# Four-layer network on one core: who issues the first row of maxima, what the first loads of an attention wait for, and when the first tokens of the grouped block are loaded

## The chip, the cores and the metric

The kernel runs on one core of a Trainium2 chip. The metric is the device time of one execution in microseconds (us); lower is better. Times of the kernel before are the median of three runs. The profile is of one further execution, and its times count from the first instruction of the span.

## The reference, cut to what matters

Four layers work on x of 4096 tokens by 128 (16 batches of 256 tokens). Each layer adds the result of an attention-like block and of an expert block to x. The change touches the attentions of the second and third layer, called att1 and att2 in the kernel, and the expert block that is run inside att1.

```python
# both attentions: 16 heads of 8
scores = einsum('bhqd,bhkd->bhqk', q, k) * scale      # att1: causal, att2: not
p = softmax(scores)
out = (einsum('bhqk,bhkd->bhqd', p, v)) @ Wo + bo
# experts beside att1: top 2 of 9
scores = sigmoid(x_flat @ gate.T + bias); top_scores, selected = top_k(scores, 2)
out += cw[:, e] * ((silu(x @ ew1[e].T) * (x @ ew3[e].T)) @ ew2[e].T)
```

## The kernel before, in words

**Stages.** Both attentions are one function, `attention`. First `projections` makes q and k in 8 chunks of 512 tokens (chunk ch holds batches 2ch and 2ch+1): TensorE multiplies, VectorE and ScalarE (ACT) split each value into three bf16 parts in a ring of PB = 4 buffers, and the queue of SyncE (SP) stores the parts of each chunk to DRAM (`q_parts`, `k_parts`, L1834), two DMAs a chunk. Their landing is counted in `stored[ch % 4]`. Between these stores, from chunk 2 to chunk 5, SP issues `early_load`: the loads of batches 0 and 1.

**Loads.** `load(b)` brings the parts of batch b back, rows arranged for TensorE: 12 DMAs (L1983 and L1985, two halves of six), into one of BUFS = 4 buffers of `qs` and `ks`.

**Steps.** The main loop has a step for each pair of heads, 8 steps a batch (PAIRS = 8), from step -12 (LEAD = 12). TensorE's step i does `scores(i)` (L2156), `maximum(i + 12)` (L2131, L2138 with the causal mask) and the product with the values of an earlier step (L2180). VectorE reduces the scores of `maximum` to row maxima (L2313 causal, L2317 not). When the 8 steps of a batch are reduced, the maxima are split in two bf16 parts, turned by TensorE (L2214) and copied by ACT to `mt` (L2295, which counts `mt_ready`). Two DMAs, together called `top(b)`, then write them into two rows of `qs` on either half (L2074), and `scores(8b)` waits for both. ACT's exponent (L2272) follows each `scores`. So before step 0 TensorE needs `top(0)`; at step 4 it needs `load(2)`, at step 12 `load(3)`.

**SP's program in the main loop** is in order: the last stores, a wait for the landing of the stores of all chunks (L1841), `load(2)`, `top(0)`, then for each batch b `top(b + 1)`, for b = 0 `load(3)`, a wait until the scores of batch b are done, and `load(b + 4)`.

**The grouped block.** In att1 the tokens are scattered by expert to `disp` by GpSimd (POOL), 64 indirect DMAs (L913). When step 32 is reached (MID = 32), all engines turn to the 72 tiles of `grouped`: SP loads a tile of 128 tokens into one of two buffers `xin` (L1177), TensorE turns it (L1226 and L1228 for tiles 0 and 1, L1190 for the rest), multiplies it with the weights of its expert (L1197), turns the gated product (L1219) and multiplies again (L1206). TensorE's order is up(0), then for each tile j: up(j + 1), turn of tile j + 2, turn of h(j), down(j - 1). SP loads tile j + 2 when tile j is turned. In SP's program this stands in the round b = 3, behind `top(4)` and `load(7)`. In att2 a dense expert block stands at MID; its code is not touched.

**What shares memory.** The buffers of `projections` are given free before `pr`, `ot` and the like are laid out, so nobody may write those before the last stores have landed. Before, SP's wait at L1841 gives this, since nothing else of the main loop can pass `top(0)`.

Of the kernel before, what the change touches and what calls it, by code (L numbers as in the profile page):

```python
# [13 lines left out]
P = 128  # L14
# [3 lines left out]
NT = N // P  # L18
# [1131 lines left out]
def grouped(nc, g, s, sb, disp, ybuf, r, w13, w2):  # L1150


    NJ = TILES1
    xin = sb("xin", [P, 2, D])
# [7 lines left out]
    def each(eng, body):  # L1162
# [6 lines left out]
        body(NJ - 2, NJ // 2 - 1, 0, 2, 1)  # L1169
        body(NJ - 1, NJ // 2 - 1, 1, 2, 0)  # L1170

    def sync(sp):
        sp.wait_ge(r.scattered, 2 * NT * 16)

        def body(j, it, p, before, after):
            sp.wait_ge(s.turned, j + 1)
            sp.dma_start(xin[:, p, :], disp[bass.ds(j * P, P), :]).then_inc(x_in[p], 16)  # L1177
        each(sp, body)

    def tensor(pe):  # L1180
        pe.sem_inc(s.turned, 2)
# [115 lines left out]

    job = Names()
    job.sync, job.tensor, job.scalar, job.vector, job.gpsimd = sync, tensor, scalar, vector, gpsimd
    return job  # L1300


# [516 lines left out]
def projections(nc, g, s, sb, w, b, q_parts, k_parts, early_load):  # L1819
# [3 lines left out]
    NCH = N // CH  # L1823
    EARLY, PB = 2, 4
# [5 lines left out]
    def sync(sp):  # L1830
        for ch in range(NCH):
            sp.wait_ge(s.p_low, ch + 1)
            for m, out in ((0, q_parts), (1, k_parts)):
                sp.dma_start(out[:, :, ch * CH:(ch + 1) * CH].rearrange("a r t -> r a t"),  # L1834
                             parts[:, ch % PB, 3 * m:3 * m + 3]).then_inc(stored[ch % PB], 16)
            if ch == EARLY:
                sp.wait_ge(stored[0], 32)
            if EARLY <= ch < EARLY + 4:
                early_load(sp, (ch - EARLY) // 2, (ch - EARLY) % 2)
        for p in range(PB):  # L1840
            sp.wait_ge(stored[p], len(range(p, NCH, PB)) * 32)  # L1841

    def tensor(pe):
        pe.wait_ge(s.p_w_in, 64)
# [71 lines left out]

    job = Names()
    job.sync, job.tensor, job.vector, job.scalar = sync, tensor, vector, scalar
    return job


def attention(nc, g, title, prologue, project, wv, bv, wo, bo, q_parts, k_parts, causal, scale, moe=None, disp=None,
# [7 lines left out]
    BUFS = 4  # L1930
# [19 lines left out]
    with section(nc, title, *names, *PROJECT, "w_in", "filled", "ones_set", "consts", "biased", "qk_in0", "qk_in1", "qk_in2", "qk_in3",  # L1950
# [109 lines left out]

        steps = range(-LEAD, NP + PAIRS)

        with nc.Block() as block:

            @block.sync
            def _(sp):
                def load(b):
                    for half in range(2):
                        load_half(sp, b, half)

                def top(b):
                    sp.wait_ge(s.mt_ready, b + 1)
                    for half in range(2):
                        sp.dma_start(qs[half * HR + KR:half * HR + KM, b % BUFS],  # L2074
                                     mt[half * 2 * PAIRS:(half + 1) * 2 * PAIRS, b % 2, :]
                                     ).then_inc(mx_in[b % 2], 16)

                parts.sync(sp)
                load(2)
                top(0)  # L2080
                for b in range(BATCH - 1):
                    top(b + 1)
                    if b == 0:
                        load(3)
                    if b == 1 and dense:
                        job.weights(sp)
                    if b + BUFS < BATCH:
                        sp.wait_ge(s.s_ready, (b + 1) * PAIRS)
                        load(b + BUFS)
                    if (moe or dense) and (b + 1) * PAIRS == MID:  # L2090
                        job.sync(sp)

# [168 lines left out]
            def _(act):  # L2261
# [17 lines left out]
                for step in steps:  # L2279
# [11 lines left out]
                    if 0 <= b + 1 < BATCH and j == TURN:  # L2291
                        act.wait_ge(s.turned_nm, b + 2)
                        if b >= 1:
                            act.wait_ge(mx_in[(b + 1) % 2], (b - 1) // 2 * 32 + 32)
                        nc.scalar.copy(mt[:, (b + 1) % 2, :], g.ps[0:4 * PAIRS, MISC, 0:T]).then_inc(s.mt_ready, 1)  # L2295

            @block.vector
            def _(dve):
# [576 lines left out]
```

## Time and profile before

| | |
|---|---|
| median of three runs | 2017.84 us (2017.4 to 2018.54) |
| the profiled execution | 2014.04 us, its span 2012.1 us |
| TensorE | busy 1563.5 us, 78% of the span |
| VectorE, ACT, GpSimd | 67%, 52%, 40% of the span |
| att1, from its projections to its end, with the grouped block | about 857 to 1368 us |
| att2, the same, with the dense block | about 1386 to 1750 us |

A row of a timeline gives the start, how long the row lasts, engine, line, operation, output and inputs, and how many instructions are merged into it; in brackets stand the idle time ahead of it and what ended it. SPq is the queue of SyncE: the time of its row is that of issuing, not of moving the data. Tiles are named att_ in both layers.

### The profile page before, as it was taken

How to read it: one execution, taken by the hardware profiler on the slowest of the kernel's cores; microseconds unless marked ns; L12 is line 12 of the kernel's file. 1: busy time of each engine (PE TensorE's matmuls, PEld its weight loads, DVE VectorE, ACT ScalarE, POOL GpSimd, SP SyncE). 2: the span in 40 equal slices, each digit the busy share in tenths (PEclk: the TensorE clock that was granted, in tenths of full speed). 3: DMA queues.
4: the chain of work that ended last, by engine and by line, in shares of the span. 5: the costliest groups of instructions: out<-in, count | busy, mean ns of one | idle time of the engine just before them, and what ended most of it. 6: DMA issues, size and time to landing. Idle time of an engine off the chain costs nothing. (4 is left out here: it accounts for less than half of the span.)

```text
span 2012.1 us, 35698 instructions
## 1 busy us (share of the span) xinstructions
PE 1563.5 (78%) x12141; PEld 1070.2 (53%) x12143; DVE 1340.9 (67%) x2371; ACT 1045.9 (52%) x1858; POOL 799.5 (40%) x803
## 2 busy tenths in 40 slices
PE   5986887887866567457788889994589999649994
PEld 5753665665644444425566666662245444437883
DVE  7537777787899998685433348868762699436334
ACT  1468778787754454144333336664354577434440
POOL 1575556555688885276011124331500000024005
PEclk9997999999987888578899999997689999769997
DMA  5211111110010010565311115522651242111322
GB/s 149 93 62 51 55 45 34 50 50 29 19 31 25 24 24 9 214 201 106 55 43 44 43 39 91 87 40 70 131 86 55 38 66 37 54 51 40 100 69 78
DMA packets 153319, 130.35 MB, mean 65 GB/s; under 512 B 18929, under 2 KB 137864, under 8 KB 152914
## 3 DMA queue, kind: packets, MB, share of 16 engines
q1 hardware_dynamic: 140626, 104.57, 21.1%
q0 software_dynamic: 12544, 23.82, 4.5%
q8 instruction: 90, 1.47, 0.3%
q14 instruction: 59, 0.48, 0.1%
HBM read 77.08 MB, written 52.43 MB: 64 GB/s over the span
## 5 line engine op out<-in xcount | busy, mean ns | idle before, releaser
L662 POOL TENSOR_TENSOR xn_t<-xn_t,scan_du 128x512 f32<-128x512 f32 x256 | 321.5, 1270 | 179.0 <-ACT xn_t L804 101.3
L707 PE MATMUL banks<-scan_hc,ident 128*128 128x256 f32 x1024 | 297.4, 417 | 73.7 <-DVE scan_hc L859 73.5
L853 DVE TENSOR_TENSOR_SCAN xn_t<-banks,xn_t 128x512 f32<-128x512 f32 x256 | 311.5, 1217 | 41.3 <-ACT banks L794 35.0
L2272 ACT ACTIVATE att_pr<-banks 128x768 f32<-128x768 f32 (+1 forms) x256 | 234.3, 916 | 139.2 <-PE banks L2164 80.3
L794 ACT ACTIVATE banks<-delta,scan_exp_centre,a_neg 128x255 f32<-128x255 f32 x512 | 265.2, 559 | 47.3 <-DVE xn_t L853 47.0
L707 PEld LDWEIGHTS banks<-scan_hc,ident 128*128 128x128 f32 x1024 | 194.1, 208 | 136.2 <-DVE scan_hc L859 101.7
L859 DVE TENSOR_TENSOR scan_hc<-xn_t,banks 128x512 f32<-128x512 f32 x256 | 175.8, 687 | 28.1 <-PE banks L692 16.1
L2317 DVE TENSOR_REDUCE att_mb<-banks 128x4 f32<-128x1024 f32 x128 | 154.0, 1222 | 25.0 <-PE banks L2131 20.2
L913 POOL DMA_INDIRECT disp<-xn_tok,places x128 | 135.3, 1057 | 86.0 <-issue 61.2
L2180 PE MATMUL banks<-att_pr,att_vx 128*32 128x256 f32 (+1 forms) x2048 | 155.0, 376 | 4.9 <-ACT att_ot L2277 3.5
L2313 DVE TENSOR_REDUCE att_mb<-banks 128x6 f32<-128x768 f32 x128 | 121.6, 956 | 40.1 <-PE banks L2138 38.2
L2131 PE MATMUL banks<-att_ks,att_qs 48*128 48x256 bf16 (+1 forms) x1024 | 112.9, 278 | 38.4 <-DMA att_ks<-k_parts 33.9
L804 ACT COPY xn_t<-banks 128x512 f32<-128x512 f32 x128 | 74.6, 583 | 129.8 <-PE banks L683 125.0
L1103 POOL IOTA route_rev<- 128x16 f32 (+2 forms) x3 | 0.4, 143 | 342.0 <-SPq L1119 316.6
L1197 PE MATMUL banks<-grouped_w,att_xt 128*128 x288 | 106.3, 493 | 32.6 <-DVE att_h L1267 31.9
L2156 PE MATMUL banks<-att_qs,att_ks 50*128 50x256 bf16 (+1 forms) x1024 | 109.3, 270 | 25.2 <-DMA att_qs<-att_mt 23.0
L1293 POOL DMA_DIRECT2D ybuf<-att_yo x72 | 38.8, 539 | 214.0 <-DVE att_yo L1274 209.9
L1241 ACT ACTIVATE att_a<-banks 128x352 f32<-128x352 f32 x72 | 33.4, 463 | 153.6 <-PE banks L1197 153.6
L1261 DVE COPY att_xt<-banks 128x128 f32<-128x128 f32 x72 | 20.9, 292 | 126.1 <-PE banks L1190 117.0
L1482 POOL DMA_INDIRECT gau_gb<-ybuf,rows x32 | 33.3, 1040 | 125.7 <-PEq L1623 119.0
L1197 PEld LDWEIGHTS banks<-grouped_w,att_xt 128*128 128x128 f32 x288 | 50.0, 193 | 62.3 <-issue 47.5
L2156 PEld LDWEIGHTS banks<-att_qs,att_ks 50*128 50x128 bf16 x1024 | 40.0, 95 | 80.7 <-issue 40.5
(342 smaller groups left out, 3348.1 us busy)
## 6 DMA issues: line engine op xcount, KB each, us to landing
scan_ew<-f_packed SPq DMA_DIRECT2D x12, 578.0 KB, 4.2
q_parts<-att_p_parts SPq DMA_DIRECT2D x16, 384.0 KB, 4.1
k_parts<-att_p_parts SPq DMA_DIRECT2D x16, 384.0 KB, 6.0
att_qs<-q_parts SPq DMA_DIRECT2D x64, 96.0 KB
att_ks<-k_parts SPq DMA_DIRECT2D x64, 96.0 KB
gau_ew<-f_packed SPq DMA_DIRECT2D x8, 578.0 KB, 4.1
disp<-zeros SPq DMA_DIRECT2D x1, 4608.0 KB, 15.9
att_xin<-disp SPq DMA_DIRECT2D x72, 64.0 KB, 1.8
```

What stands on the lines that cost most here:

```text
L662: nc.gpsimd.tensor_tensor(bu[:, i % RING], b_sb[:, q % 2], du[:, b % 2, c:c + 1, :].to_broadcast([P, 2, T]), ALU.mult).then_inc(s.bu_made, 1)
L707: ins = nc.tensor.matmul(bank(Y_BANK)[:, c, :], g.ident[:], hc[:, i % RING, n, :], start=False, stop=(i % (PAIRS * DC) == PAIRS * DC - 1 a ...
L794: ins = nc.scalar.activation(bank(DA + i % RING)[:, n, 1:T], delta[:, c, b * T + 1:(b + 1) * T], ACT.Exp, scale=a_neg[:, c, state:state + ...
L853: v.tensor_tensor_scan(rows(h[:, i % 2]), g.ps[:, DA + i % RING, :], rows(bu[:, i % RING]), 0.0, ALU.mult, ALU.add).then_inc(s.scan_done, 1)
L859: v.tensor_tensor(hc[:, i % RING], h[:, i % 2], bank(C_BANK), ALU.mult).then_inc(s.hc_ready, 1)
L913: pool.indirect_dma_start(disp, bass.IndirectOffsetOnAxis(ap=r.scat_i[:, k, i:i + 1], axis=0), src[:, i, :], None, bounds_check=disp.shape ...
L1197: ins = nc.tensor.matmul(g.ps[:, 4 * p + 1 + m, 0:H1], xt[:, p, :], rows(w13[:, bass.ds(e, 1), m * H1:(m + 1) * H1]), start=True, stop=True)
L2156: ins = nc.tensor.matmul(g.ps[:, 2 * s_slot(i) + half, k * T:k * T + T - q0], ks[rows_of, p, j, k * P:(k + 1) * P], qs[rows_of, p, j, q0:T ...
L2180: ins = nc.tensor.matmul(g.ps[r * 32:(r + 1) * 32, O_BANK, q0:T], vx[:, b % 2, k, 4 * jg + r, :], pr[:, i % RING, half, k * T:k * T + T - q0],
L2272: nc.scalar.activation(pr[:, i % RING], g.ps[:, at:at + 2, 0:W], ACT.Exp, scale=scale).then_inc(s.p_ready, 1)
L2313: v.tensor_reduce(mb[:, b % 2, j, :].rearrange("p (g n) -> p g n", g=2), g.ps[:, at:at + 2, 0:W].rearrange("p g (n k) -> p g n k", k=P), A ...
L2317: v.tensor_reduce(mb[:, b % 2, j, :], g.ps[:, at:at + 2, :].rearrange("p g (n k) -> p (g n) k", k=T), AX_X, ALU.max).then_inc(s.m_taken, 1)
```

## The change

In both attentions ACT issues `top(0)` itself, behind its copy that makes `mt` of batch 0, and then waits until the stores of all chunks have landed. SP no longer waits for all stores: ahead of each `load(b)` with even b it waits for the stores of chunk b / 2 alone. In att1 SP loads tiles 0 and 1 of the grouped block in the round b = 2 (behind `load(6)`, once all scattered rows have landed), and in the round b = 3 only the loop for tiles 2 to 71 is left.

```diff
+    def first_tokens(sp):
+        sp.wait_ge(r.scattered, 2 * NT * 16)
+        for j in range(2):
+            sp.dma_start(xin[:, j, :], disp[j * P:(j + 1) * P, :]).then_inc(x_in[j], 16)
+
     def sync(sp):
-        sp.wait_ge(r.scattered, 2 * NT * 16)
-
-        def body(j, it, p, before, after):
+        def body(j, p):
             sp.wait_ge(s.turned, j + 1)
             sp.dma_start(xin[:, p, :], disp[bass.ds(j * P, P), :]).then_inc(x_in[p], 16)
-        each(sp, body)
+
+        with sp.Fori(1, NJ // 2) as it:
+            for p in range(2):
+                body(it * 2 + p, p)
...
-        for p in range(PB):
-            sp.wait_ge(stored[p], len(range(p, NCH, PB)) * 32)
+
+    def chunk_stored(eng, ch):
+        eng.wait_ge(stored[ch % PB], (ch // PB + 1) * 32)
+
+    def all_stored(eng):
+        for ch in range(NCH - PB, NCH):
+            chunk_stored(eng, ch)
...
+        def top(eng, b):
+            eng.wait_ge(s.mt_ready, b + 1)
+            for half in range(2):
+                eng.dma_start(qs[half * HR + KR:half * HR + KM, b % BUFS],
+                              mt[half * 2 * PAIRS:(half + 1) * 2 * PAIRS, b % 2, :]).then_inc(mx_in[b % 2], 16)
...
                 def load(b):
+                    if b % 2 == 0:
+                        parts.chunk_stored(sp, b // 2)
                     for half in range(2):
                         load_half(sp, b, half)
...
                 parts.sync(sp)
                 load(2)
-                top(0)
                 for b in range(BATCH - 1):
-                    top(b + 1)
+                    top(sp, b + 1)
                     if b == 0:
                         load(3)
...
                         load(b + BUFS)
+                    if moe and (b + 2) * PAIRS == MID:
+                        job.first_tokens(sp)
                     if (moe or dense) and (b + 1) * PAIRS == MID:
                         job.sync(sp)
...
                         nc.scalar.copy(mt[:, (b + 1) % 2, :], g.ps[0:4 * PAIRS, MISC, 0:T]).then_inc(s.mt_ready, 1)
+                        if b == -1:
+                            top(act, 0)
+                            parts.all_stored(act)
```

## Rows read from the trace of the kernel before

**Rows 1.** The page, its head.

```profile
span 2012.1 us, 35698 instructions
```

**Rows 2.** The waits of TensorE in att1 (857 to 1368): total, times, longest.

```profile
PE banks L2131 <- DMA att_ks<-k_parts: 17.4, 3, 11.9
...
PE banks L2156 <- DMA att_qs<-att_mt: 10.7, 1, 10.7
PE banks L1226 <- DMA att_xin<-disp: 9.1, 1, 9.1
```

**Rows 3.** The same view of att2 (1386 to 1750).

```profile
PE banks L2156 <- DMA att_qs<-att_mt: 12.3, 2, 9.2
```

**Rows 4.** Timeline of SP's queue at the start of att1.

```profile
896.08 1.24 SPq L1834 DMA_DIRECT2D k_parts<-att_p_parts  x1
903.11 0.32 SPq L1983 DMA_DIRECT2D att_qs<-q_parts  x1
...
908.62 16.16 SPq L2074 DMA_DIRECT2D att_qs<-att_mt  x4
```

**Rows 5.** Timelines of ACT and of TensorE there: end of step -1, step 0, step 4.

```profile
900.48 0.36 ACT L2295 CAST att_mt<-banks 32x256 bf16<-32x256 f32 x1 [10.40 <-PE banks L2214]
...
902.73 0.37 PE L2138 MATMUL banks<-att_ahead_k,att_half_eye 64*128 64x128 bf16 x4
913.81 0.39 PE L2156 MATMUL banks<-att_qs,att_ks 50*128 50x256 bf16 x2 [10.70 <-DMA att_qs<-att_mt]
...
920.77 0.22 PE L2131 MATMUL banks<-att_ks,att_qs 48*128 48x128 bf16 x2
```

**Rows 6.** Timelines of SP's queue, ACT and TensorE at the start of att2.

```profile
1428.50 0.31 SPq L1983 DMA_DIRECT2D att_qs<-q_parts  x1
...
1434.62 14.76 SPq L2074 DMA_DIRECT2D att_qs<-att_mt  x4
...
1427.11 0.36 ACT L2295 CAST att_mt<-banks 32x256 bf16<-32x256 f32 x1 [10.83 <-PE banks L2214]
...
1428.70 0.61 PE L2131 MATMUL banks<-att_ks,att_qs 48*128 48x256 bf16 x4
1438.53 0.61 PE L2156 MATMUL banks<-att_qs,att_ks 50*128 50x256 bf16 x4 [9.22 <-DMA att_qs<-att_mt]
```

**Rows 7.** Timelines of SP's queue and of TensorE's weight loads: `top(1)` of att1.

```profile
923.51 1.26 SPq L2074 DMA_DIRECT2D att_qs<-att_mt  x2
...
926.17 0.10 PEld L2156 LDWEIGHTS banks<-att_qs,att_ks 50*128 50x128 bf16 x2 [0.20 <-DMA att_qs<-att_mt]
```

**Rows 8.** Timeline of all engines where the grouped block starts.

```profile
968.14 0.30 SPq L1983 DMA_DIRECT2D att_qs<-q_parts  x1
...
969.49 0.42 DVE L2382 TENSOR_TENSOR x_tok<-x_tok,banks 128x256 f32<-128x256 f32 x1
...
972.99 20.27 SPq L1177 DMA_DIRECT2D att_xin<-disp  x8
...
978.53 0.45 PE L1226 MATMUL banks<-ident,att_xin 128*128 128x128 f32 x1 [9.08 <-DMA att_xin<-disp]
...
979.71 5.06 PE L1197 MATMUL banks<-grouped_w,att_xt 128*128 x8 [0.52 <-DVE att_xt L1261]
...
984.56 0.37 PE L1190 MATMUL banks<-ident,att_xin 128*128 128x128 f32 x1
...
988.22 1.45 PE L1197 MATMUL banks<-grouped_w,att_xt 128*128 x4 [0.26 <-DVE att_h L1267]
```

**Rows 9.** Windows of 1 us: busy time by engine, then PEclk, DMA share, GB/s.

```profile
901.00:902.00 1.00, 1.00 (x10) 0.87 (x4) 1.00 (x2) 0.00 (x0) 0.70 (x2) 0.50 0.61 218
...
971.00:972.00 1.00, 0.00 (x0) 0.00 (x0) 0.00 (x0) 0.00 (x0) 0.00 (x0) 0.55 0.77 81
```

**Rows 10.** Timelines of GpSimd and SP's queue: the last scatter, the end of `load(6)`.

```profile
946.30 0.97 POOL L913 DMA_INDIRECT disp<-xn_tok,places  x1 [0.30 <-issue]
...
960.28 0.31 SPq L1985 DMA_DIRECT2D att_ks<-k_parts  x1
```

More of the change, by code:

```diff
@@ L1299, in grouped @@
     job.sync, job.tensor, job.scalar, job.vector, job.gpsimd = sync, tensor, scalar, vector, gpsimd
+    job.first_tokens = first_tokens
     return job
@@ L1918, in projections @@
     job.sync, job.tensor, job.vector, job.scalar = sync, tensor, vector, scalar
+    job.chunk_stored, job.all_stored = chunk_stored, all_stored
     return job
@@ L2067, in load @@
                 def load(b):
+                    if b % 2 == 0:
+                        parts.chunk_stored(sp, b // 2)
                     for half in range(2):
                         load_half(sp, b, half)
[L2071 to L2076, printed above, removed]
                 parts.sync(sp)
                 load(2)
-                top(0)
                 for b in range(BATCH - 1):
-                    top(b + 1)
+                    top(sp, b + 1)
                     if b == 0:
```

## The prediction, as it was written before the result was known

> **What bounds the kernel now.** I read the page first: TensorE is the busiest engine, at 78% (the table above), so time is gained only where it stands idle in the stages that the change touches, and then only as much as nothing later takes back. [rows 1] gives the span against which the sum is made. Then the waits of TensorE by stage. In att1 three waits for a transfer stand out: 17.4 us for the loads of keys (11.9 of it ahead of the first maxima), 10.7 us in one piece for the row of maxima `top(0)`, and 9.1 us in one piece for the first tokens of the grouped block [rows 2]. In att2 the wait for `top(0)` is 9.2 us [rows 3]. The change aims at the 10.7, the 9.1 and the 9.2: 29.0 us at most, 1.4% of the span. The reader is to see that each is a single hole on the engine that sets the pace, so a us taken out of it is a us of the end, until the next wait is met.
>
> Then the timelines around each hole, to see what the transfer itself was late for. In att1 ACT has `mt` ready at 900.48 + 0.36 = 900.84, and TensorE is through with step -1 at 903.1 [rows 5]. SP issues the last store until 897.32, waits for its landing, issues `load(2)` from 903.11, and only behind its 12 DMAs `top(0)` at 908.62; the row merges it with `top(1)` [rows 4]. TensorE goes on at 913.81. So of the hole, 7.8 us are SP being late to issue (908.62 - 900.84), and 5.2 us are issue and landing. In att2 the same: ready at 1427.47, TensorE through at 1429.3, `load(2)` from 1428.50, `top(0)` at 1434.62, TensorE on at 1438.53 [rows 6].
>
> **Edit 1, `top(0)` from ACT.** ACT has nothing else before the first exponent. Price of the pair of DMAs where the queue is quiet: `top(1)` of att1 is issued 923.51 to 924.77 and TensorE's weight load is released by it at 926.17, so 1.26 us of issue and 1.4 of landing [rows 7]. Behind the traffic of `load(2)` the landing was 913.81 - (908.62 + 1.26) = 3.9 us in att1 [rows 4, 5] and 1438.53 - 1435.88 = 2.65 us in att2 [rows 6]. On ACT the issue in att1 would be at 900.9 to 902.2. The trace has no DMA from ACT, so its landing is bounded: 1.4 us (quiet) gives 903.6; waiting until what SP has queued is moved gives about 910 (next part). The transfers are not quiet there: the DMA engines are 61% busy at 901 with stores [rows 9], and `load(2)` comes behind. I take the middle of 1.4 and 3.9 (2.7) and 0.4 more for two queues issuing at once: 905.3. That is 8.5 us ahead of 913.81; TensorE is free at 903.1, so nothing of it is lost. In att2 the issue is at 1427.5 to 1428.8, the landing between 1430.2 and 1434.5; the tail of the stores is over sooner here, so I take 3.0 us: 1431.8, that is 6.7 us ahead of 1438.53.
>
> By the Trainium skill (DMA: Bandwidth & Descriptors, Queues, rings and completion order) SP and ACT each have a ring of their own on each of the same DMA engines, which take turns between rings packet by packet; by that the two small DMAs would pass SP's backlog, which is the side that I take. The same page (Issuing engines are not separate DMA queues) says that issuing from more engines saves only the sequencer's time to issue. No row here shows ACT issuing; what it would make is the first rival.
>
> **Edit 2, `load(2)` without the wait for the last stores.** It is issued from 897.4 instead of 903.11, 5.7 us sooner (in att2, where the code is the same, about as much). By itself this fills no hole: TensorE asks for it at step 4, which is 920.77 - 913.81 = 7.0 us after step 0 [rows 5]. With step 0 at 905.3 that is 912.3, so without edit 2 (`load(2)` landed by about 913.8) edit 1 would lose 1 to 2 us there. How soon it lands now: a whole load with two token tiles behind it takes from 968.14 to 978.5, 10.4 us [rows 8]. Behind the stores, which hold the DMA engines until about 902 [rows 9], it lands between 909 (issued until about 903.5, and 5.5 us of tail, as 972.99 to 978.5) and 912.5 (902 and 10.4). So it is hidden, or costs 0.2 us. What waits behind: `top(1)` and `load(3)` come with the maxima of batch 1, at the same distance from step 0 as before; the 2.6 us that TensorE waits for `load(3)` at step 12 stay. ACT's new wait for all stores (landed by 903.1) ends before it could have an exponent to do; behind it is queued only that exponent. Nothing is gained or lost by it. In between, steady steps are paced by TensorE, so the shift is kept to MID.
>
> **Edit 3, tokens of tiles 0 and 1 in round b = 2.** Before, TensorE could start at about 969.9 (VectorE's last sum of the first batches, 969.49 + 0.42) and starts at 978.53, since both tiles are issued behind the 12 DMAs of `load(7)` and their data [rows 8]. With the tiles there, turning tiles 0 and 1 and the products of both take 4.0 us at the clock that the pair of 1.45 us shows, so TensorE asks for tile 2 at 974. But tile 2 is now what stands behind `load(7)`: issued at 972.99, landed at 978.5, as tile 0 was. The hole shrinks from 9.1 to 4.5 us; the saving read at tile 2 is 984.56 - 978.5 = 6.1 us. From this goes the clock. Here 8 products took 5.06 us after the hole and later 4 took 1.45 [rows 8]; the granted clock had fallen to 1.2 GHz at about 971.5, 2 us after TensorE fell idle [rows 9], and it was back at 2.4 GHz only some 6 us after work began again. Before, those 6 us were tiles 0 and 1; now they are tiles 2 and 3: from the turn of tile 2 to the end of that of h(1), 2.7 us at the high clock, about 5.4 at the low one, so 2.7 to 3.0 us are given back. Net 3.1 us, with 1.5 and 6.1 as ends.
>
> What SP is held by now: the wait for the scattered rows comes at 960.6 - 8.5 = 952 instead of 973. The last scatter is issued until 947.3 [rows 10], and a few us of landing are covered. Behind the wait stand `top(4)`, needed only after the grouped block, and `load(7)`, issued at 959.6 at the soonest. So it costs nothing unless the scatter lands after 959.6. The loop for tiles 2 to 71 changes two unrolled ends into rounds of the loop; each load waits for TensorE's turn anyhow.
>
> **Sum.** 8.5 + 6.7 + 3.1 = 18.3 us of 2014.04 in the profiled execution, which would be 1995.7; its span plus 1.9 us. The median of the runs is 3.8 us above that execution, and the same 18.3 from 2017.84 gives 1999.5.
>
> **The rivals.**
> *Behind the same backlog.* `top(0)` from ACT is not served ahead of SP's. Then it lands with `load(2)`: the data of `load(2)` could start only when the stores let them, some 2 to 4 us sooner than before. I take 3.5 in each attention, with 3.1 at MID: 10.1, so 2007.7. For it: landing already grew from 1.4 to 3.9 us behind a load. Against: that was on one queue. The second sentence of the Trainium skill above would come out this way.
> *The grouped block gives nothing.* The hole only moves to tile 2 and the slow clock eats the rest: 15.2, so 2002.6.
> *More than I count.* Quiet landing in both (10.2 and 8.3) and a clock that is not lost at MID (6.1): 24.6, so 1993.2.
> *Held by the scatter.* If the scattered rows land after 959.6, the first tokens come as before: 15.2, the same number.
> *The change doesn't do what it says.* If the first DMAs of a queue that has not been used so far land no sooner than 913.8 and 1438.5, only MID is left, or less: 2015 to 2018.
> *Slower.* The same place, with a price: ACT's first exponent and TensorE's step 0 both hang on the two DMAs that ACT issues. If a first issue from ACT takes over 13 us from 900.84 (11 us from 1427.47 in att2), the attention starts later than before; at 20 us, as if something had to be fetched for it, it costs 7 and 9 us less the 3.1 of MID: 2031. Nothing in the profile speaks for it, since SP's DMAs have no such first cost here.
>
> **How the numbers follow.** Forecast (14 to 21 us saved, with small misses of either kind) 0.60. Backlog 0.14. Grouped block nothing, or held 0.09. More 0.10. No effect 0.04. Slower 0.03. The likeliest gives 1999.5. The range must reach to the quiet bound and to the backlog: 1993 to 2008. A measurement of this kernel tells 0.2% (4 us) from no change. Faster 0.93, within 0.2% 0.04, slower 0.03.
>
> **What would show it.** Right: two DMAs from ACT about 0.1 us behind its copy of `mt` in each attention; TensorE's wait at L2156 down from 10.7 to 2 or 3 us and from 9.2 to 2 or 3; no new wait over 1 us at L2131 in step 4; the wait at L1226 gone and one of 4 to 5 us at L1190 for tile 2, with the products of tiles 2 and 3 at the low clock. Wrong: ACT's row of maxima landing over 5 us after issue; a wait for keys at step 4 that gives back what the row won; the wait at L1190 as long as that at L1226 was.

## The result and the profile after

| | before | after |
|---|---|---|
| median of four runs | 2017.62 us (2015.63 to 2018.54) | 2003.33 us (1997.86 to 2006.37) |
| the profiled execution | 2014.04 us, span 2012.1 | 1997.86 us, span 1995.9 |

The ratio is 0.9946 (95% interval 0.9926 to 0.9967): 14.3 us by the medians, inside the range of the prediction, faster as in its likeliest case, and 3.8 us above its time. The profiled execution of after is the quickest of its four, so the stages have to be read one by one.

From the page of after: its head, and the group of `scores` (busy time and mean | idle time ahead and what ended most of it).

```profile
span 1995.9 us, 35718 instructions
...
L2171 PE MATMUL banks<-att_qs,att_ks 50*128 50x256 bf16 (+1 forms) x1024 | 108.2, 268 | 16.3 <-DMA att_qs<-att_mt 14.4
```

TensorE still waits 14.4 us for rows of maxima. The waits of TensorE in att1 of after (840 to 1370), in total, times and longest, answer to [rows 2]:

```profile
PE banks L2146 <- DMA att_ks<-k_parts: 18.3, 3, 12.1
PE banks L2171 <- DMA att_qs<-att_mt: 6.0, 2, 5.5
PE banks L1196 <- DMA att_xin<-disp: 4.5, 1, 4.5
```

and those in att2 (1350 to 1750) to [rows 3]:

```profile
PE banks L2146 <- DMA att_ks<-k_parts: 16.7, 3, 11.8
PE banks L2171 <- DMA att_qs<-att_mt: 8.4, 3, 4.9
```

The hole ahead of step 0 fell from 10.7 to 5.5 us and from 9.2 to 4.9, not to the 2 or 3 that were forecast. Timelines of SP's queue, ACT and TensorE at the start of att1 of after, beside [rows 4, 5]:

```profile
895.53 0.98 SPq L1841 DMA_DIRECT2D k_parts<-att_p_parts  x1
896.55 1.12 SPq L1996 DMA_DIRECT2D att_qs<-q_parts  x1
...
903.20 0.31 SPq L1998 DMA_DIRECT2D att_ks<-k_parts  x1
...
900.12 0.36 ACT L2310 CAST att_mt<-banks 32x256 bf16<-32x256 f32 x1 [10.31 <-PE banks L2229]
900.51 1.90 ACTq L2079 DMA_DIRECT2D att_qs<-att_mt  x2
...
908.25 0.39 PE L2171 MATMUL banks<-att_qs,att_ks 50*128 50x256 bf16 x2 [5.50 <-DMA att_qs<-att_mt]
...
913.76 0.22 PE L2146 MATMUL banks<-att_ks,att_qs 48*128 48x128 bf16 x2
...
930.48 0.23 PE L2146 MATMUL banks<-att_ks,att_qs 48*128 48x128 bf16 x2 [2.91 <-DMA att_ks<-k_parts]
```

The reader is to see the order of issue. `load(2)` now starts at 896.55, 4.0 us ahead of ACT's first DMA, and by 900.5 six of its twelve DMAs have been begun. ACT does issue 0.03 us behind its copy, until 902.41, and step 0 begins at 908.25: landing took 5.8 us. That is the prediction's own sign of being wrong ("ACT's row of maxima landing over 5 us after issue"), and it came in both attentions. Windows of the same stretch (busy time by engine, then PEclk, DMA share, GB/s; the window 901 of before is in [rows 9]) show why it was not quiet:

```profile
902.00:903.00 1.00, 0.74 (x12) 0.47 (x12) 0.64 (x2) 0.00 (x0) 0.69 (x2) 0.50 0.94 157
...
907.00:908.00 1.00, 0.00 (x0) 0.00 (x0) 0.00 (x0) 0.00 (x0) 0.70 (x2) 0.50 0.41 113
```

The DMA engines are full, with the load and at first the last stores, and the row is there when they have all but drained: the last data of `load(2)` landed at 908.74, 0.5 us behind the row's (from the increments of its semaphore in the trace). Step 4 (913.76) finds its keys; step 12 waits 2.91 us for `load(3)`, as before. In att2 the same (SP, ACT, TensorE; beside [rows 6]): by ACT's first DMA ten of the twelve have been begun, ACT's issue ends at 1421.32, and landing takes 5.4 us.

```profile
1414.82 1.16 SPq L1996 DMA_DIRECT2D att_qs<-q_parts  x1
...
1420.82 0.55 SPq L1998 DMA_DIRECT2D att_ks<-k_parts  x1
...
1419.60 0.36 ACT L2310 CAST att_mt<-banks 32x256 bf16<-32x256 f32 x1 [10.83 <-PE banks L2229]
1419.99 1.33 ACTq L2079 DMA_DIRECT2D att_qs<-att_mt  x2
...
1426.68 0.61 PE L2171 MATMUL banks<-att_qs,att_ks 50*128 50x256 bf16 x4 [4.88 <-DMA att_qs<-att_mt]
```

The start of the grouped block (beside [rows 8]): the timeline of all engines, then two windows.

```profile
955.58 1.22 SPq L1175 DMA_DIRECT2D att_xin<-disp  x2
...
964.50 0.42 DVE L2400 TENSOR_TENSOR x_tok<-x_tok,banks 128x256 f32<-128x256 f32 x1
...
965.33 0.30 PE L1232 MATMUL banks<-ident,att_xin 128*128 128x128 f32 x1 [0.87 <-DVE x_tok L2400]
...
966.42 2.63 PE L1203 MATMUL banks<-grouped_w,att_xt 128*128 x8 [0.69 <-DVE att_xt L1267]
...
968.29 9.72 SPq L1180 DMA_DIRECT2D att_xin<-disp  x4
...
973.60 0.48 PE L1196 MATMUL banks<-ident,att_xin 128*128 128x128 f32 x1 [4.55 <-DMA att_xin<-disp]
...
974.58 2.71 PE L1203 MATMUL banks<-grouped_w,att_xt 128*128 x4
```

```profile
971.00:972.00 1.00, 0.00 (x0) 0.00 (x0) 0.00 (x0) 0.00 (x0) 0.00 (x0) 0.85 0.60 65
972.00:973.00 1.00, 0.00 (x0) 0.00 (x0) 0.00 (x0) 0.00 (x0) 0.00 (x0) 0.50 0.50 54
```

The first tokens are there, eight products run at the high clock (2.63 us), and the hole is now the 4.55 us at tile 2, behind `load(7)`. The clock falls in it from 2.4 to 1.2 GHz, so the next four products take 2.71 us, against 1.45 at the high clock in [rows 8].

**Stages.** One ruler serves all kernels below, read from the timelines: att1 runs from ACT's first copy of `mt` (900.48 before, 900.12 after) to VectorE's last sum ahead of the grouped block (969.49, 964.50); the block from there to the turn of its last tile (1191.91, 1182.98); att2 from its copy of `mt` (1427.11, 1419.60) to SP's first load of the dense block's packed weights (`att_fw`), which stands behind `top(2)` (1469.57, 1458.42).

| us | att1 | block | att2 |
|---|---|---|---|
| before | 69.0 | 222.4 | 42.5 |
| after | 64.4 | 218.5 | 38.8 |
| saved | 4.6 | 3.9 | 3.7 |

That is 12.2 us. The span shows 16.2; the other 4.0 lie in stretches where no instruction was changed, and 3.6 of them in one: from the load of the packed weights to ACT's copy of `mt` of the sixth batch of att2. Windows of that stretch in before, after and after_again, a second profile of after with a span of 2002.0:

```profile
1469.57:1589.03 119.46, 110.73 (x632) 54.50 (x628) 53.47 (x76) 60.89 (x87) 0.00 (x0) 0.94 0.27 57
1458.42:1574.32 115.90, 107.28 (x640) 53.61 (x632) 53.57 (x76) 61.10 (x87) 0.00 (x0) 0.99 0.27 59
1459.84:1578.68 118.84, 110.10 (x628) 54.30 (x624) 53.03 (x76) 60.56 (x87) 0.00 (x0) 0.94 0.26 57
```

The mean granted clock was 0.94, 0.99 and 0.94: one execution of after kept the high clock there, and the other, of the same kernel, did not and took 2.9 us more. So these 3.6 us cannot be put down to the change.

### The profile page after: what moved, and what is told of

Read it like the earlier page. It is cut to its first block and busy times, and to the rows that moved or that the text cites. A ratio compares the mean times of both kernels' runs of the same rounds, so it can differ in the third digit from the quotient of the medians.

```text
span 1995.9 us, 35718 instructions
## 1 busy us (share of the span) xinstructions
PE 1557.2 (78%) x12142; PEld 1066.5 (53%) x12143; DVE 1340.7 (67%) x2371; ACT 1046.1 (52%) x1858; POOL 800.3 (40%) x803
## 5 line engine op out<-in xcount | busy, mean ns | idle before, releaser
L913 POOL DMA_INDIRECT disp<-xn_tok,places x128 | 136.0, 1063 | 85.0 <-issue 61.2
L2335 DVE TENSOR_REDUCE att_mb<-banks 128x4 f32<-128x1024 f32 x128 | 153.8, 1221 | 19.5 <-PE banks L2146 14.7
L2331 DVE TENSOR_REDUCE att_mb<-banks 128x6 f32<-128x768 f32 x128 | 121.5, 956 | 35.3 <-PE banks L2153 33.6
L1299 POOL DMA_DIRECT2D ybuf<-att_yo x72 | 38.8, 539 | 205.4 <-DVE att_yo L1280 201.2
L2171 PE MATMUL banks<-att_qs,att_ks 50*128 50x256 bf16 (+1 forms) x1024 | 108.2, 268 | 16.3 <-DMA att_qs<-att_mt 14.4
L217 PE MATMUL banks<-ident,xn_tok 128*128 128x128 f32 x128 | 34.3, 427 | 59.8 <-DVE xn_tok L186 59.8
```

Source lines behind the costliest of these rows:

```text
L913: pool.indirect_dma_start(disp, bass.IndirectOffsetOnAxis(ap=r.scat_i[:, k, i:i + 1], axis=0), src[:, i, :], None, bounds_check=disp.shape ...
L2331: v.tensor_reduce(mb[:, b % 2, j, :].rearrange("p (g n) -> p g n", g=2), g.ps[:, at:at + 2, 0:W].rearrange("p g (n k) -> p g n k", k=P), A ...
L2335: v.tensor_reduce(mb[:, b % 2, j, :], g.ps[:, at:at + 2, :].rearrange("p g (n k) -> p (g n) k", k=T), AX_X, ALU.max).then_inc(s.m_taken, 1)
```

## The experiments

Each is an edit of the kernel after. `sp` is SP's program. The rival explanations were that ACT's queue has a price of its own, or that the row waits for, or shares the DMA engines with, what SP has issued.

### First set: each edit alone, and the row with nothing beside it

**a_row_from_act**, edit 1 alone.

```diff
                 parts.sync(sp)
+                parts.all_stored(sp)
                 load(2)
...
-                    if b % 2 == 0:
-                        parts.chunk_stored(sp, b // 2)
```

`first_tokens` stands in the round b = 3 again, as in the next kernel.

> Edit 1 alone: ACT issues top(0), SP waits for all stores ahead of load(2) as before, tokens of tiles 0 and 1 loaded as before. Theory 1 (the row from ACT queues with what SP has queued: in the changed kernel load(2) kept it for 5.8 us behind its issue in att1, 5.4 in att2): here load(2) isn't queued yet when the row is issued, only the tail of the stores is, so the row lands 1.4 to 4 us behind its issue; TensorE's wait for the row falls to 1 to 3 us in each attention, and about 2 us of it come back at step 4 as a wait for load(2), which is as late as before. 12 to 15 us saved. Theory 2 (ACT's own queue has a price of its own, about 5 us, whatever else is queued): the waits for the row stay at about 5.5 and 5 us, as in the changed kernel, nothing at step 4, and about 9 us are saved.

**b_loads_own_chunk**, edit 2 alone.

```diff
                 load(2)
+                parts.all_stored(sp)
+                top(sp, 0)
...
-                            top(act, 0)
-                            parts.all_stored(act)
```

> Edit 2 alone: SP issues load(2) once its own chunk is stored, then waits for all stores and issues top(0) itself; tokens as before. Theory 1 (the data of load(2), not the issuing, holds the row): top(0) is issued at about 903.2 in att1 and lands with the data of load(2) at about 908, as late as the row from ACT did in the changed kernel; wait for the row about 5 to 6 us in att1 and in att2; 8 to 10 us saved, so edit 1 added little to it. Theory 2 (ACT's queue is slow, SP's would be quick): the row lands 1.4 to 2.6 us behind its issue, at 906; 12 us saved.

**c_first_tokens**, edit 3 alone: SP waits for all stores, then `load(2)`, `top(sp, 0)`.

> Edit 3 alone: only the tokens of tiles 0 and 1 move to the round b = 2. As in the changed kernel: the wait at the turn of tile 0 is gone, one of 4.5 us stands at the turn of tile 2, the turn of tile 2 comes 6 us sooner and the last tile 3.8 us sooner, because 2.2 us go to the low clock. 3 to 4 us saved. Rival: the 3.8 us need the shift of the first part too (the scatter has to be over, SP has to be ahead): then less than 2.

**d_row_lands_first**, all three, and `load(2)` held until the row is there.

```diff
                 parts.sync(sp)
+                sp.wait_ge(mx_in[0], 32)
                 load(2)
```

> The changed kernel, but SP issues load(2) only when both DMAs of the row have landed. Theory 1: nothing but the stores is ahead of the row, it lands 1.4 to 3 us behind its issue (TensorE waits 1 to 2 us for it instead of 5.5 and 4.9); load(2) is issued at 904 to 910 and lands at about 913, so that step 4 waits 1 to 3 us for it; 1 to 3 us faster in each attention than the changed kernel at best, or the same. Theory 2: the row lands 5 to 6 us behind its issue all the same, load(2) is issued only at 908 and lands at 917 to 918, step 4 waits 3 us for it: about 3 us slower in each attention than the changed kernel.

These ran on another chip, where the kernel before took 2134.55 us. All four have holes of TensorE there that no other chip showed: from the first maxima to the first copy of `mt` in att1 it is 67 to 69 us, and 11 to 12 in all other profiles; the last section tells of them. Behind them nothing of SP's is in flight when the row is issued, so att1 could show nothing of edits 1 and 2, and att2 and the block are the places to read.

| | median, us | ratio to before, 95% interval | att1 | block | att2 | copy to step 0 in att2 |
|---|---|---|---|---|---|---|
| a, edit 1 | 2129.72 | 0.9972 (0.9957 to 0.9986) | 58.0 | 221.9 | 36.2 | 4.5 |
| b, edit 2 | 2128.21 | 0.9978 (0.9960 to 0.9995) | 58.3 | 222.0 | 38.8 | 7.9 |
| c, edit 3 | 2130.76 | 0.9982 (0.9966 to 0.9999) | 57.5 | 218.9 | 42.5 | 11.2 |
| d | 2132.56 | 0.9992 (0.9975 to 1.0008) | 65.0 | 219.0 | 39.0 | 3.1 |

Edit 1 alone, in att2 (ACT, SP's queue, TensorE):

```profile
1549.15 0.36 ACT L2309 CAST att_mt<-banks 32x256 bf16<-32x256 f32 x1 [10.82 <-PE banks L2228]
1549.55 1.32 ACTq L2079 DMA_DIRECT2D att_qs<-att_mt  x2
...
1550.46 0.31 SPq L1996 DMA_DIRECT2D att_qs<-q_parts  x1
...
1553.68 0.61 PE L2170 MATMUL banks<-att_qs,att_ks 50*128 50x256 bf16 x4 [2.33 <-DMA att_qs<-att_mt]
```

Here the load comes behind the row, and the row lands 2.8 us behind its issue: the price that the prediction took (in i below, in the same place and the same order, 1.7). Edit 1 alone is worth 6.3 us in att2 (42.5 less 36.2; c, where att2 is that of before, has 42.5 on this chip too), the forecast's 6.7. Edit 2 alone, where the row is issued by SP at 1550.18 to 1551.60, behind a load that began 6.5 us earlier, and step 0 starts at 1555.61, is worth 3.7. Both together gave 3.7 in after, so they don't add: once edit 2 is in, edit 1 brings next to nothing. (The medians, 4.8 us for a and 6.3 for b, do not rank the two: their intervals overlap widely.) Edit 3 alone is worth 3.5 us in the block against before, 3.0 to 3.1 against a and b on the same chip, and 3.8 by the medians.

The quiet price of a row from ACT is in d, att2: issue until 1552.09, step 0 at 1553.45, 1.4 us, as for SP in [rows 7]. So ACT's queue shows no price of its own. What d paid is the load: `load(2)` began only 3.0 us behind the copy in att2 and 3.6 in att1, and TensorE met it at step 4. In att1 of d:

```profile
1034.05 0.29 PE L2147 MATMUL banks<-att_ks,att_qs 48*128 48x128 bf16 x2 [3.02 <-DMA att_ks<-k_parts]
```

with 2.98 at step 12 (2.1 to 2.8 in a, b and c): att1 was 7 us longer than in a, b and c, where the load had long landed. The two waits are 3.2 to 3.9 us of it; the rest is the clock. The window of d behind the wait at step 4:

```profile
1034.00:1041.00 7.00, 6.95 (x98) 4.45 (x100) 2.99 (x4) 2.25 (x4) 0.00 (x0) 0.59 0.02 5
```

The granted clock is 0.59 there; in a it is 1.00 from 1032 to 1042, the same distance behind its copy. By the stages d gives back in att1 what it won elsewhere, and by the medians it gained nothing that is clear of noise.

### Second set: edit 2 taken away, and what is issued around the row moved

**after_again**, the kernel after unchanged.

> The changed kernel, unchanged, on the chip of this job, as the reference for the three beside it. On the chip of its first run it saved 16.2 us of the span. If this chip has the three long holes of TensorE at the start of att1 that the first four experiments showed (some 65 us from the first maxima to the copy of the first row), the row and load(2) have all the time they need there and att1 gives 0 to 1 us instead of 5; then att2 gives 3.6 and the grouped block 3.8: 7 to 9 us in all. Without those holes 13 to 16.

**i_edits_1_and_3**, after without edit 2: the two changes of a, with `first_tokens` in the round b = 2.

> The changed kernel without edit 2: SP waits for all stores ahead of load(2) again. Theory 1 (load(2), queued in front of the row, holds it): the row lands 2.8 us behind its issue in att2, as with edit 1 alone, TensorE's wait for it is 2.3 instead of 4.9 us, nothing is asked back at step 4 in att2; 2 to 3 us faster than the changed kernel in att2. In att1, if there are no long holes, the row is in time at 904, but step 4 waits 1 to 2 us for load(2): 2 to 3 us faster there too; with the long holes no difference. Rival: edit 2 is worth something of its own when step 4 comes sooner: then a wait for keys of 2.5 us or more stands at step 4 and the two kernels are equal.

**g_load3_early**

```diff
                 load(2)
+                load(3)
                 for b in range(BATCH - 1):
                     top(sp, b + 1)
-                    if b == 0:
-                        load(3)
```

> The changed kernel with load(3) right behind load(2), ahead of top(1). It tells how the row from ACT is served. If the row takes turns with SP's queue on the DMA engines, one more load behind load(2) does not move it: wait for the row 4.9 us in att2 as before, and the wait of 2.9 us for load(3) at step 12 is gone in both attentions: 3 to 6 us faster than the changed kernel. If the row is served only when SP's queue is drained, it lands 7 to 8 us later than in the changed kernel, a wait of 12 us in att2 and, without the long holes, in att1: 5 to 9 us slower.

**f_load7_behind_block**: in the round b = 3 `job.sync(sp)`, the loads of tiles 2 to 71, stands ahead of the wait for the scores and `load(7)`.

> The changed kernel with load(7) behind the loads of the whole grouped block instead of ahead of tile 2. If load(7) is what tile 2 waited for: the wait of 4.5 us at the turn of tile 2 is gone (tile 2 is loaded when tile 0 is turned and lands 1.8 us later), the clock stays at its high level, and the grouped block ends 6 to 7 us sooner than in the changed kernel. load(7) is issued at the end of the block and is needed 12 steps later, some 16 us, so nothing is asked back. Rival: it is late there: a wait for keys of several us at step 44 and less than 3 us gained.

### Third set: the row from SP, and the gains together

**e_row_from_sp_first**

```diff
                 parts.sync(sp)
+                top(sp, 0)
                 load(2)
...
-                            top(act, 0)
```

> All three edits, but the first row of maxima is issued by SP again, ahead of the second batch's load; ACT keeps the wait for all stores. Theory 1 (the row shares the DMA engines with whatever has been queued ahead of it; which engine issues it does not matter): the row has only the tail of the stores ahead of it, lands 1.3 to 2.8 us behind its issue, and scores(0) start 3.5 to 4.5 us after the copy of the maxima in both attentions (after: 7.6 to 8.1 and 7.1 to 7.6). The load is issued some 1.3 us behind the copy, so TensorE waits up to 1.5 us for keys at step 4. The stage from the copy to the grouped block is then 61 to 62.5 us (after 65.3), the one in att2 35 to 36.5 (after 39), and the time about 6 us under that of after, some 1993 to 1996. Theory 2 (passing the backlog needs a queue of its own): the row lands 4 us or more behind its issue as on SP before, scores(0) start at 6 us or later, and the time is that of after. Theory 3 (the load becomes the hole): a wait of 3 us or more at step 4, and nothing gained over after.

**k_sp_first_load3_early**: e with the edit of g.

> The kernel of the run before this one, with the load of batch 3 issued right behind that of batch 2, so SP's order is row 0, load(2), load(3), row 1. Theory 1: the wait of 2.9 us at step 12 goes in both attentions, but row 1 now stands behind 24 DMAs that begin only at the copy: it is issued some 14 us after it and step 8 asks for it some 17 us after it, so a wait of 0 to 3 us at step 8 takes the place of the one at step 12. The stages are 59 to 62 us in att1 and 33 to 36 in att2; the time is 0 to 6 us under that of the run before. If the gains add (row first: 6 us, load(3) early: 7 us under after), the time is near 1987; if row 1 is late, it is no better than load(3) early alone (ratio 0.990 to before).

**gf_load3_early_load7_late**: after with the edits of g and f.

> All three edits with the row issued by ACT, load(3) right behind load(2), and load(7) behind all tile loads of the grouped block. Theory 1 (gains of different places add): att1's first stage about 61.3 us, the grouped block 211 us instead of 217.5, att2's stage 34.5. Of the 6.5 us of the block up to 3.4 are given back at the end of it, where TensorE waits 1.4 us for VectorE's output and the clock falls; so the time is 3 us under load(3) early alone, ratio about 0.9885. Rival: the give-back takes all of it, and the ratio is 0.990, as for load(3) early alone.

**h2_combined**: e with the edits of g and f.

> Row 0 from SP ahead of load(2), load(3) right behind load(2), load(7) behind all tile loads. Theory 1: as the second run of this call in the attentions, with the block at 211 us and up to 3.4 us given back behind it: 3 us under that run, ratio 0.985 to 0.988. Rival: the late load(7) gives nothing that is kept, and the ratio is that of the second run of this call.

Before took 2012.05 us (11 runs) beside the second set and 2014.97 us (11 runs) beside the third, each set on one chip. The column "rest" runs from the last tile's turn to att2's copy (before 235.2); "copy to step 0" is that of att1, then att2 (before 13.3 and 11.4).

| | median, us | ratio to before, 95% interval | att1 | block | rest | att2 | copy to step 0 |
|---|---|---|---|---|---|---|---|
| after_again | 2000.09 | 0.9937 (0.9922 to 0.9953) | 64.6 | 218.1 | 234.7 | 39.4 | 7.8, 7.6 |
| i, no edit 2 | 1998.81 | 0.9932 (0.9917 to 0.9947) | 61.2 | 218.1 | 234.8 | 35.9 | 3.6, 3.4 |
| g, load(3) early | 1992.58 | 0.9899 (0.9883 to 0.9914) | 60.4 | 218.9 | 234.7 | 34.5 | 9.3, 7.8 |
| f, load(7) late | 1998.82 | 0.9925 (0.9907 to 0.9944) | 65.3 | 211.9 | 238.1 | 38.5 | 7.3, 7.1 |
| e, row from SP | 1996.42 | 0.9913 (0.9891 to 0.9935) | 63.9 | 218.2 | 237.1 | 35.3 | 3.3, 3.2 |
| k = e + g | 1993.68 | 0.9898 (0.9877 to 0.9920) | 62.9 | 218.7 | 235.2 | 39.6 | 3.4, 3.2 |
| gf | 1986.31 | 0.9857 (0.9833 to 0.9880) | 59.9 | 211.8 | 237.2 | 35.5 | 8.3, 8.5 |
| h2 = e + g + f | 1990.76 | 0.9872 (0.9850 to 0.9894) | 62.8 | 211.9 | 237.2 | 37.9 | 3.3, 3.2 |

**The row waits for what was issued ahead of it.** Without edit 2 (i), ACT's row again has nothing of the load ahead of it. Timelines of ACT, SP's queue and TensorE in att1 of i:

```profile
901.13 1.91 ACTq L2079 DMA_DIRECT2D att_qs<-att_mt  x2
...
903.29 0.32 SPq L1996 DMA_DIRECT2D att_qs<-q_parts  x1
...
904.37 0.40 PE L2170 MATMUL banks<-att_qs,att_ks 50*128 50x256 bf16 x2 [1.01 <-DMA att_qs<-att_mt]
...
912.88 0.23 PE L2145 MATMUL banks<-att_ks,att_qs 48*128 48x128 bf16 x2 [1.27 <-DMA att_ks<-k_parts]
```

Landing takes 1.3 us, and the stages of both attentions are 3.4 and 3.5 us shorter than in after_again: edit 2 takes back about half of what edit 1 brings. (The medians show 1.3 us of these 7, and the intervals of the two ratios overlap; the profile of i is of the quickest of its six executions, that of after_again of one of the two slowest. That the row lands earlier is shown, that the kernel is quicker is not.) In g twelve more DMAs stand behind `load(2)`, and the row comes 1.5 us later than in after_again in att1 and 0.2 later in att2. In att1 of g:

```profile
911.32 0.39 PE L2170 MATMUL banks<-att_qs,att_ks 50*128 50x256 bf16 x2 [6.63 <-DMA att_qs<-att_mt]
```

`load(3)` was issued until 10 and 7 us behind the copy and landed at 14.9 and 12.3 us, so the row, at 9.3 and 7.8, did not wait for all that SP had queued. But `load(3)` is no part of the backlog ahead of the row: its first DMA was issued 3.8 and 1.8 us behind the copy, when ACT had issued both of the row's (by 2.3 and 1.7). What stood ahead was `load(2)` alone. For every kernel and attention in which all or half of it did, these are the times behind the copy, in us, of the end of issue and of the last data (the last increment of each semaphore in the trace):

| | row issued by | row's issue ends | issue of `load(2)` ends | row landed | `load(2)` landed |
|---|---|---|---|---|---|
| before, att1 | SP | 9.7 | 8.1 | 13.3 | 12.5 |
| before, att2 | SP | 8.9 | 7.5 | 11.4 | 11.0 |
| c, att2 | SP | 9.7 | 8.2 | 11.1 | 10.9 |
| b, att2 | SP | 3.9 | 2.2 | 7.8 | 7.5 |
| gf, att2 | ACT | 1.7 | 1.4 | 8.5 | 8.0 |
| after_again, att2 | ACT | 1.7 | 1.4 | 7.6 | 7.4 |
| after, att2 | ACT | 1.7 | 1.8 | 7.0 | 7.2 |
| f, att2 | ACT | 1.7 | 1.8 | 7.0 | 7.2 |
| g, att2 | ACT | 1.7 | 1.8 | 7.8 | 8.2 |
| after, att1 | ACT | 2.3 | 3.4 | 8.1 | 8.6 |
| f, att1 | ACT | 2.3 | 3.0 | 7.3 | 8.0 |
| after_again, att1 | ACT | 2.3 | 3.4 | 7.7 | 8.6 |
| g, att1 | ACT | 2.3 | 3.8 | 9.2 | 10.3 |
| gf, att1 | ACT | 2.3 | 5.4 | 8.2 | 10.6 |

Whichever engine issues the row, it lands with `load(2)`: 0.2 to 0.8 us behind it where the row's issue ends later, 0.2 to 1.1 us before it where the load's last DMAs were issued within 1.5 us of the row's, and 2.4 us before it where they came 3.1 us later (gf, att1). This is the order of issue, across both queues, and it is the prediction's first rival. The DMA queues of the trace show the waiting itself. q10 is ACT's queue: after has 72 packets on it, before none. Queues of after in 1419.60 to 1424.15 (from the copy), then in 1424.15 to 1426.00, then of i in 1414.92 to 1417.80 (packets, MB, share of the 16 engines):

```profile
q1 hardware_dynamic: 1131, 0.55, 78.5%
```

```profile
q10 hardware_dynamic: 36, 0.02, 5.2%
```

```profile
q10 hardware_dynamic: 36, 0.02, 2.0%
```

In after ACT issues from 1419.99 to 1421.32, and not one of its 36 packets is moved by 1424.15, while SP's queue moves 1131. In i all 36 are moved within 2.5 us of ACT's first issue. The Trainium skill (DMA: Bandwidth & Descriptors, Queues, rings and completion order) has the DMA engines take turns between the queues; by that the row would have passed, and in this case it did not, so here the measurement decides. Where the order is kept, in the DMA engines or ahead of them, no run shows. The same page (Issuing engines are not separate DMA queues) has an issue from another engine save only the sequencer's time; e agrees: a row issued by SP ahead of the load starts step 0 3.3 and 3.2 us behind the copy, one by ACT in i 3.6 and 3.4. What matters is what was issued ahead of the row, not who issues it.

**In att1 the next hole is the load.** In e the load begins 2.0 us behind the copy, so step 4 meets it. SP's queue and TensorE, att1 of e:

```profile
902.57 1.52 SPq L2079 DMA_DIRECT2D att_qs<-att_mt  x2
904.13 0.43 SPq L1996 DMA_DIRECT2D att_qs<-q_parts  x1
...
905.43 0.28 PE L2172 MATMUL banks<-att_qs,att_ks 50*128 50x256 bf16 x2 [0.63 <-DMA att_qs<-att_mt]
...
914.44 0.23 PE L2147 MATMUL banks<-att_ks,att_qs 48*128 48x128 bf16 x2 [4.06 <-DMA att_ks<-k_parts]
```

Step 0 came 4.5 us sooner after the copy than in after_again, and 4.06 us of it went at step 4, with the clock behind it (granted 1.00 until 914, 0.61 on average from 914 to 918); att1 as a whole won 0.7 us where 3 to 4 were expected. In att2 the first steps are longer: TensorE asks for the load some 8 us behind step 0 (11.4 less 3.1 us after the copy in d), in att1 of e after 5 (8.2 less 3.3). So there is no wait at step 4, and 4.1 of 4.4 us stay. In k the load of batch 3 then holds back row 1, and step 8 waits instead. TensorE in att1, then att2 of k:

```profile
925.06 0.28 PE L2171 MATMUL banks<-att_qs,att_ks 50*128 50x256 bf16 x2 [2.37 <-DMA att_qs<-att_mt]
...
1442.18 0.61 PE L2171 MATMUL banks<-att_qs,att_ks 50*128 50x256 bf16 x4 [3.91 <-DMA att_qs<-att_mt]
```

So the row ahead of the load and `load(3)` early undo each other in att2: k's 39.6 is after's. What makes `load(3)` early pay in g and gf is edit 2: the loads start 3.5 us and more before the row, and the wait at step 12 is gone without a new one at step 8 over 0.6 us. There edit 2 earns what it did not earn in after.

**The block.** With `load(7)` behind the tiles (f), TensorE does not wait at tile 2 and keeps the high clock; the block is 6.3 us shorter. Some is given back where the block ends, for TensorE waits there for VectorE (timeline of f), and the clock falls (windows of 20 us of f, then of after, each from 5 us ahead of the last tile's turn):

```profile
1189.68 0.40 PE L2173 MATMUL banks<-att_qs,att_ks 50*128 50x256 bf16 x2 [1.43 <-DVE att_yo L1280]
```

```profile
1176.00:1196.00 20.00, 16.70 (x156) 11.59 (x155) 6.71 (x15) 7.79 (x18) 5.33 (x8) 0.83 0.40 69
```

```profile
1178.00:1198.00 20.00, 17.73 (x226) 12.42 (x225) 9.61 (x24) 9.39 (x20) 6.42 (x10) 1.00 0.10 32
```

The rest is 238.1, 237.2 and 237.2 in the three kernels with that edit and 235.5 on average (234.7 to 237.1) in after's two profiles, i, g, e and k: so about 2 us go back, though the spread of the others is as large. Some 4 us stay by the stages, and gf, with both edits, has the lowest median: 1986.31 us, ratio 0.9857, against 0.9899 for g alone, beside other runs of before. h2, which has the row from SP as well, is 4.5 us slower by the median, and the two intervals overlap.

**How far the stages account for the medians.** From att1's copy to the end of the att2 stage, the savings on before are 12.2 us in after_again, 19.0 in i, 20.7 in g, 15.3 in f, 14.6 in e, 12.6 in k, 24.7 in gf and 19.2 in h2; the medians say 12.0, 13.2, 19.5, 13.2, 18.6, 21.3, 28.7 and 24.2. All but i and k agree within 5 us; the intervals reach 3 to 5 us to either side. i's profile is of its quickest execution, 4.4 us under its median. k is 8.7 us off, and its profile is of its slowest execution (2000.0 us; the quickest took 1992.35). What differed between the executions of one kernel is not settled beyond the one stretch above.

## Why the prediction was right, and where it was not

The time lay in the range, and the three places were the right ones. The mechanism of the likeliest case, a row from ACT that passes SP's load, is not what the kernel does.

**What bounds the kernel: right.** The three holes were the place. Of their 29.0 us, 14.9 are left as waits (5.5, 4.55 and 4.88). One reading is loose: the 7.8 us of late issue and the 5.2 of issue and landing are parts of the 13.0 us from `mt` to step 0, not of the hole of 10.7, since TensorE was busy until 903.1; the sum does not use them.

**Edit 1: the landing was mis-sized, and for a reason.** ACT issued as forecast, and by itself the edit is worth 6.3 us in att2 (forecast 6.7), with landing at 2.8 us (forecast 3.1 in att1, 3.0 in att2). In after the term "I take the middle of 1.4 and 3.9 (2.7) and 0.4 more for two queues issuing at once" was mis-sized: 5.8 and 5.4 us. The 3.9 was read from a row behind its own queue's load and then halved towards the quiet 1.4, as if another queue passed the load. It does not, and edit 2 had put six DMAs of the load ahead of the row in att1 and ten in att2: the row landed with the load. Saved up to step 0 were 5.2 us of 8.5 and 4.3 of 6.7 (13.3 less 8.1, 11.4 less 7.1).

**Edit 2: the step that failed.** "By itself this fills no hole", and the sum has no term for it; that is wrong on both sides. Alone it is worth 3.7 us in att2 (b), since SP reaches `top(0)` sooner; the prediction did not price it alone. Beside edit 1 it costs 3.4 and 3.5 us by the stages (i against after_again), since it puts the load ahead of the row. What it was credited with, the keys at step 4, was right in small: step 4 found them, and without edit 2 (i) TensorE waits 1.3 us there in att1, though not in att2. With the two terms at 4.6 and 3.7 the attentions gave 8.3 us of 15.2.

**Edit 3: right, a little under.** 3.9 us in after's profile, 4.3 in after_again, 3.0 to 3.5 alone, for 3.1. The hole at tile 2 was 4.55 us (forecast 4.5), at the low clock as said. The scatter did not hold SP: the tokens were issued at 955.58.

**The rivals.** "Behind the same backlog" forecast 3.5 us in each attention, and by size it is nearer (4.6 and 3.7; 4.4 and 3.0 in after_again) than the forecast is. As a mechanism it is what the runs show: "Then it lands with `load(2)`" holds within 0.9 us in after and after_again, and a load issued behind the row (g) is no test against it. Its bound of "about 910" for att1 was 908.2. Its chance of 0.14 was too small beside 0.60. The rival in which the clock eats the block's gain and the slow rival did not come.

**Why the time was near all the same.** 1999.5 was forecast, 2003.33 measured, 2000.09 on a chip whose before was 5.6 us quicker. The stages saved 12.2 us and the medians 14.3 and 12.0, for 18.3 forecast and 10.1 in the backlog rival. The sum was a third too high. 2003.33 lies about as near the rival's 2007.7 (4.4 us) as the forecast's 1999.5 (3.8): the medians saved 2.1 us more than the stages, which is within their interval, and on the other chip nothing more. The range held the time by its lower half of savings, which it had for the backlog's sake. That the likeliest time came so near, with the landing mis-sized by 2.7 and 2.4 us in the two attentions, is in part luck.

## What to carry to other kernels

Two edits that each take time out of the same hole are not to be summed: price each with the other in place, by writing down what is issued ahead of the critical transfer in the new order, from whatever engine. Here a second queue did not pass the first: the row landed with the load that had been issued ahead of it, from ACT as from SP. A small transfer that one engine waits for wants to be issued ahead of a big one, but only so far as the big one's own due time allows; here the best order was to start both loads as early as their data allowed and accept a wait of some 6 us for the row (5.6 to 6.6 in g and gf). A new wait costs more than its length where the clock falls in it (d, e). A load that is issued in front of a short stage can be put behind that stage's own transfers if its user comes much later.

## What the runs showed that was not expected

On the chip of the first set every kernel with a profile had long holes in att1 between its first maxima and the first copy of `mt`. Waits of TensorE in a, 930 to 1060:

```profile
PE banks L2145 <- DVE att_mb L2330: 38.4, 3, 21.1
...
PE banks L2152 <- issue: 12.6, 10, 2.6
PE banks L2145 <- issue: 6.7, 2, 4.4
```

The same wait for `att_mb` is 0.5 us in all in att1 of e, k and gf, on another chip, and the median of before was some 120 us higher there: the stretch is 57 us longer, and the projections of att1 began 63 us later (921.3 us in a, 858.0 in before). VectorE stood idle in the holes too, and the profile names nothing in the kernel that it waited for. "issue" is time in which the profile shows nothing to wait for; the cause stays open. An experiment on the start of a stage is worth little on such a chip, while stages further on read as elsewhere: the kernel with edit 3 alone has a block of 218.9 us there, and after one of 218.5 and 218.1 on others.

A hole costs clock as well. In after TensorE does no more work from about 969.1 until 973.60, and the windows show a granted clock of 1.00 until 971, 0.85 from 971 to 972, and 0.50 in the next. The hole of 4.55 us thus cost another 1.3 us in the first four products behind it (2.71 against 1.45). And a stretch that no edit touched, in the dense block of att2, took 115.9 us at a mean clock of 0.99 and 118.8 to 119.5 at 0.94: a single profile can hold 3 to 4 us that belong to no edit.
